# A Perceiver block on one core: the experts' first block prepared while self-attention drains

## What is computed

```python
x = x + cross_attention(layernorm(x), ctx, ctx, mask)      # 257 keys a batch, 16 heads
x = x + self_attention(layernorm(x))                       # 32 keys a batch, 16 heads
x = x + moe(layernorm(x))

def moe_layer(x, rw, rb, g, b, w1, b1, w2, b2):            # four of these in a row
    probs = softmax(x @ rw + rb)                           # 4 experts
    vals, idx = top_k(probs, 2); vals = vals / vals.sum()
    xhat = layernorm(x)
    xe = xhat * g[e] + b[e]                                # own gain and offset per expert
    h = gelu(xe @ w1[e] + b1[e])                           # 128 -> 512, exact gelu
    expert_out[e] = x + h @ w2[e] + b2[e]                  # 512 -> 128
    return sum over e of comb[e] * expert_out[e]           # all four are computed, two weigh
```

## Time and profile before

| | us |
|---|---|
| median of 3 executions | 1393.75 |
| lowest, highest | 1386.02, 1393.91 |
| the profiled execution | 1394.39 |
| its span, first to last instruction | 1391.7 |
| PE busy (share) | 1292.1 (93%) |
| DVE busy | 1167.6 (84%) |
| ACT busy | 1114.4 (80%) |
| POOL busy | 712.9 (51%) |

### The profile page before, as it was taken

How to read it: one execution, slowest core, us unless ns; L and a number is a source line. 1 busy time by engine, 2 the same in 40 slices (tenths; PEclk the granted TensorE clock), 3 DMA queues, 4 the chain that set the end, 5 groups by cost and what they waited for, 6 DMA issues and landing times.

```text
span 1391.7 us, 45724 instructions
## 1 busy us (share of the span) xinstructions
PE 1292.1 (93%) x15671; PEld 976.8 (70%) x15671; DVE 1167.6 (84%) x3416; ACT 1114.4 (80%) x1886; POOL 712.9 (51%) x557
## 2 busy tenths in 40 slices
PE   5898999999997699986999999999999999999998
PEld 3676778778776588843767667777777777777776
DVE  4799988999998689887999988788878887889885
ACT  3598999999996657655898978888888888888886
POOL 7276777777776865531444433333333333333333
PEclk9899999999998679997999999999999999999999
DMA  5875766766763288800000000000000000000000
GB/s 157 231 211 161 188 187 181 191 185 186 195 172 90 42 216 219 220 14 1 2 1 0 0 1 1 0 0 0 0 0 0 0 0 0 2 8 15 8 17 16
DMA packets 196207, 108.54 MB, mean 78 GB/s; under 512 B 89740, under 2 KB 194028, under 8 KB 196076
## 3 DMA queue, kind: packets, MB, share of 16 engines
q1 hardware_dynamic: 122032, 84.65, 21.9%
q10 hardware_dynamic: 74044, 22.17, 7.2%
HBM read 67.62 MB, written 39.03 MB: 77 GB/s over the span
## 4 chain that ended last, share of the span: by engine, by line
PE 46%; DVE 3%; issue 2%; ACT 1%; DVEq 0%; ACTq 0%
PE pair L1787 22%; PE pair L1769 20%; PE pair L1776 2%; PE pair L1808 1%; PE pair L1799 1%; DVE hs L1693 1%; ACT gf L1614 0%; DVE w1p L1046 0%; DVE gl L1679 0%; DVE w2p L1050 0%; DVE rw L38 0%; DVE st L1640 0%; DVE xl L1740 0%; ACT gh L1619 0%; DVE rs L53 0%
## 5 line engine op out<-in xcount | busy, mean ns | idle before, releaser
L1601 POOL TENSOR_TENSOR gl<-gf,gh 128x1024 f16<-128x1024 f32 x128 | 286.5, 2239 | 480.4 <-ACT gh L1619 480.4
L1614 ACT ACTIVATE gf<-pair,b1c 128x512 f32<-128x512 f32 x512 | 327.2, 680 | 98.3 <-PE pair L1769 97.0
L1787 PE MATMUL pair<-w2p,gh 128*128 (+1 forms) x4096 | 357.3, 219 | 0.0
L1787 PE MATMUL pair<-w2p,gl 128*128 (+1 forms) x2048 | 349.6, 219 | 0.0
L1769 PE MATMUL pair<-xh,w1p 128*128 128x512 f16 x1024 | 329.2, 383 | 9.8 <-ACT gf L1614 8.2
L1787 PEld LDWEIGHTS pair<-w2p,gh 128*128 128x128 f16 x4096 | 319.7, 98 | 23.0 <-issue 0.4
L405 POOL TENSOR_TENSOR pl<-p,ph 128x1024 f16<-128x1024 f32 x128 | 273.1, 2134 | 118.5 <-ACT ph L462 118.4
L1619 ACT ACTIVATE gh<-gf 128x1024 f16<-128x1024 f32 x256 | 270.6, 1057 | 24.0
L1679 DVE SCALAR_TENSOR_TENSOR gl<-gf,gh 128x1024 f16<-128x1024 f32 x128 | 160.8, 1256 | 83.5 <-ACT gh L1619 81.3
L1787 PEld LDWEIGHTS pair<-w2p,gl 128*128 128x128 f16 x2048 | 200.3, 98 | 0.0
L1769 PE MATMUL pair<-xl,w1p 128*128 128x512 f16 x512 | 196.1, 383 | 0.0
(11 more groups left out here) (240 smaller groups left out, 2448.8 us busy)
## 6 DMA issues: line engine op xcount, KB each, us to landing
KS<-k_parts_dram SPq DMA_DIRECT2D x64, 384.0 KB, 4.4
k_parts_dram<-kh SPq DMA_DIRECT2D x64, 256.0 KB, 3.4
cx<-in_ctx_dram ACTq DMA_DIRECT2D x30, 512.0 KB, 4.5
k_parts_dram<-kl SPq DMA_DIRECT2D x64, 128.0 KB, 3.6
w1p<-in_L_ffn_w_dram SPq DMA_DIRECT2D x8, 512.0 KB, 5.8
w2p<-in_L_ffn_w_dram SPq DMA_DIRECT2D x8, 512.0 KB, 7.6
QS<-q_parts_dram ACTq DMA_DIRECT2D x128, 24.0 KB
K<-k_parts_dram SPq DMA_DIRECT2D x8, 384.0 KB
```

The lines of the kernel that those rows point to most:

```text
L1601: pool.tensor_tensor(gl[u.m2][:, 0:h, :], gf[u.m2][:, 0:h, :], gh[u.m2][:, 0:h, :], ALU.subtract).then_inc(d_loP, 1)
L1614: act.activation(gf[u.m2][:, c, :], hb[c][:, :], ACT.Gelu, scale=1.0 / WS, bias=b1c[:, u.step.expert(u.e), c]).then_inc(d_g, 1)
L1787: last = pe.matmul(yb[v.m2][:, t * D:(t + 1) * D], g[:, c, t * P:(t + 1) * P], w2p[:, le, part, c, :].rearrange("p a h -> p (a h)"), start ...
```

## The change

It has four parts.

1. *The experts' first block in the drain.* DVE's aggregation and deviations of the first 24 tiles move two slots earlier, (7, 0) to (7, 2). ACT writes `hs` tiles 0 to 11 at the ends of slots (7, 3), (8, 0), (8, 1), tiles 12 to 15 in the prologue, and 16 to 31 in units (1, 1), (1, 3), (2, 1), (2, 3). DVE makes the moments of the first eight of these tiles in (8, 1) (`st8`, `mv8`), the deviations of steps 0 and 1 together and `xc` of step 0 in (8, 2), and PE transposes it at the end of the block. ACT issues one small GELU (`warm`) in (8, 0).
2. *The offsets' products with swapped operands.* For each expert four products with a 128x128 piece of fp32 weights as stationary and the one column of offsets as moving operand, written to where `b1c` reads them: `lnbd`, `b1r` and the transposes go. All sixteen experts are done in (6, 2) to (7, 3). The low weights of experts 0 and 1 are made by DVE in (7, 3) and (8, 0), and wait for all sixteen; those of 2 and 3 move to units (0, 0) and (0, 1).
3. *Routing behind the first unit.* In the prologue DVE only makes `xl` and `route` of step 0 and `xc` of step 1. The tanh moves behind the GELUs of unit (0, 0), `weigh` behind the low half there. `deviations(2)` is in (0, 2), behind `low_half(2)`; `attended_late` is at the end of (1, 2) and now makes only scales and biases.
4. *Steps 1 to 6 are written out* instead of looped.

```diff
-                            if at == (NBLK, 1):
-                                act.wait_ge(c_s, HEAD + 4)
-                                act.wait_ge(e_ln, HEAD + RSTD_STEPS + 1)
-                                for t in range(FIRST_HS):
-                                    attended(act, t)
-                            if at in ((NBLK, 1), (NBLK, 2)):
-                                high_weights(act, 1 + w)
...
+                            if at in ATTENDED:
+                                for t in range(*ATTENDED[at]):
+                                    attended(act, t)
+                            if at == (NBLK, 0):
+                                act.activation(warm[:, :], gain[:, 0:1], ACT.Gelu)
+                            if at in ((NBLK, 0), (NBLK, 1)):
+                                high_weights(act, 2 + w)
+                    ATTENDED = {(7, 3): (0, 4), (NBLK, 0): (4, 8), (NBLK, 1): (8, 12)}
...
-                            if at in ((7, 3), (NBLK, 1), (NBLK, 2), (NBLK, 3)):
-                                le = w % 4 if at[0] == NBLK else 0
-                                dve.wait_ge(e_b1, le + 1)
-                                low_weights(dve, le)
...
+                            if at in ((7, 3), (NBLK, 0)):
+                                le = (w + 1) % 4
+                                dve.wait_ge(e_b1, LE)
+                                low_weights(dve, le)
+                            if at == (NBLK, 1):
+
+                                dve.wait_ge(d_hs, 8)
+                                for k in range(8):
+                                    dve.bn_stats(st8[:, k, :], hs[:, k, :]).then_inc(d_ln, 1)
+                                dve.wait_ge(d_ln, 8)
+                                dve.tensor_tensor(b1c[:, :, :].rearrange("p x c -> p (x c)"), bank[1][:, 0:LE * FC],
+                                                  cols[:, 64:64 + LE * FC], ALU.add)
+                                for k in range(8):
+                                    dve.bn_aggr(mv8[:, k // 4, k % 4, :], st8[:, k, :]).then_inc(d_ln, 1)
+                            if at == (NBLK, 2):
+                                flat = lambda r: r[:, :, :].rearrange("p i k -> p (i k)")
+                                dve.wait_ge(d_ln, 16)
+                                inverse_deviation(dve, seed, flat(rs8), flat(rw8), flat(rt8),
+                                                  mv8[:, :, :, 1].rearrange("p i k -> p (i k)"), d_ln, 16)
+                                for k in range(4):
+                                    dve.tensor_scalar(xc[:, k, :], hs[:, k, :], mv8[:, 0, k, 0:1], rs8[:, 0, k:k + 1],
+                                                      ALU.subtract, ALU.mult).then_inc(d_x, 1)
...
-                                    pe.matmul(bank[1][0:LE, 0:F], lnbd[:, le, :], w1f[:, le + SHIFT, :], start=(le == 0),
-                                              stop=(le == LE - 1)).then_inc(e_b1, 1)
-                    BIAS1 = {(6, 2): (0, 1), (6, 3): (1, 2), (7, 0): (2, 3), (7, 1): (3, 4), (7, 2): (4, 6), (7, 3): (6, 8),
-                             (8, 0): (8, 10), (8, 1): (10, 12), (8, 2): (12, 14), (8, 3): (14, 16)}
+                                    for c in range(FC):
+                                        last = pe.matmul(bank[1][:, le * FC + c:le * FC + c + 1], w1f[:, le + SHIFT, c * P:(c + 1) * P],
+                                                         cols[:, 32 + le:33 + le], start=True, stop=True)
+                                    last.then_inc(e_b1, 1)
+                    BIAS1 = {(6, 2): (0, 2), (6, 3): (2, 4), (7, 0): (4, 7), (7, 1): (7, 10), (7, 2): (10, 13), (7, 3): (13, LE)}
...
-                with eng.Fori(0, SPLITS // 2) as it:
-                    for k in range(2):
-                        run(it, 1 + k, False, splits=True)
+                for s in range(1, 1 + SPLITS):
+                    run(0, s, False, splits=True)
...
-                        if f and e == 3:
-                            act.wait_ge(d_r, RSTEPS * (f.n + 1))
+                        weighed = u.step if at == (0, 0) else f if u and f and e == 3 else None
+                        if weighed:
+                            act.wait_ge(d_r, RSTEPS * (weighed.n + 1))
                             act.activation(th[:, :, :], z[:, :, :], ACT.Tanh).then_inc(d_th, 1)
...
+                    LATER = {(1, 1): (16, 20), (1, 3): (20, 24), (2, 1): (24, 28), (2, 3): (28, NT)}
...
                     def unit(u, v, f, third, e, final):
-                        if f and e == 0:
-                            if not u:
-                                deviations(f)
+                        at = (u.step.n, e) if u and isinstance(u.step.n, int) else None
+                        opening = at is not None and at[0] == 0
+                        if u and f and e == 0:
                             normalise(f, final)
-                        if third and e == 1 and u:
+                        if u and third and e == 1 and not opening:
                             deviations(third)
...
-                        if third and e == 1 and not u:
-                            deviations(third)
-                            attended_late()
                         if u:
                             low_half(u)
+                        if at == (0, 0):
+                            low_weights(dve, 2)
+                            weigh(u.step)
+                        if opening and e == 2:
+                            deviations(third)
                         if f and e == 2:
                             route(f)
                         if v:
                             combine(v, final)
...
+                        if at == (0, 1):
+                            low_weights(dve, 3)
+                        if at == (1, 2):
+                            attended_late()
```

More of the change, by code:

```diff
@@ L1060, in build @@
         e_rwh, e_b2, e_ln = sem("e_rwh"), sem("e_b2"), sem("e_ln")
-        d_acc = sem("d_acc")
+        st8 = sb(whole, "st8", [P, 8, 6], F32)
+        mv8 = sb(whole, "mv8", [P, 2, 4, 2], F32)
+        rs8, rw8, rt8 = (sb(whole, f"rs8_{i}", [P, 2, 4], F32) for i in range(3))
+        warm = sb(whole, "warm", [P, 1], F32)
+        xc = sb(whole, "xc", [P, 4, D], F32)
+        d_acc, d_hs = sem("d_acc"), sem("d_hs")
+        d_ln, d_x, d_xT = sem("d_ln"), sem("d_x"), sem("d_xT")
         def attended(act, t):
             act.activation(hs[:, t, :], xs[:, t, :], ACT.Identity, scale=rs3[:, t:t + 1],
-                           bias=nb3[:, t:t + 1]).then_inc(d_acc, E)
+                           bias=nb3[:, t:t + 1]).then_inc(d_hs, 1)
         with ExitStack() as S:
@@ L1089, in build @@
             cols = sb(S, "cols", [P, P], F32)
-            lnbd = sb(S, "lnbd", [P, LE, LE], F32)
-            b1r = sb(S, "b1r", [LE, F], F32)
             WLOAD = 16 * 2 * NBLK
@@ L1388, in step @@
                                              xs[:, bass.ds(y, 1), :].rearrange("p a c -> p (a c)")).then_inc(c_st, 1)
+                            if at in ((7, 0), (7, 1)):
+                                dve.wait_ge(c_st, NT + HEAD)
+                                for t in range(w * HEAD // 2, (w + 1) * HEAD // 2):
+                                    dve.bn_aggr(mv3[:, t, :], st2[:, t, :]).then_inc(e_ln, 1)
+                            if at == (7, 2):
+                                a = slice(0, HEAD)
+                                dve.wait_ge(e_ln, HEAD)
+                                inverse_deviation(dve, seed, rs3[:, a], rw3[:, a], rt3[:, a], mv3[:, a, 1], e_ln, HEAD)
+                                dve.scalar_tensor_tensor(nb3[:, a], mv3[:, a, 0], -1.0, rs3[:, a], ALU.mult, ALU.mult).then_inc(e_ln, 1)
@@ new lines, in step @@
+                                    last.then_inc(e_b1, 1)
+                    BIAS1 = {(6, 2): (0, 2), (6, 3): (2, 4), (7, 0): (4, 7), (7, 1): (7, 10), (7, 2): (10, 13), (7, 3): (13, LE)}
+                    blocks(step)(pe)
+                    pe.wait_ge(d_x, 4)
+                    pe.wait_ge(c_oc, NT)
+                    for k in range(4):
+                        last = pe.transpose(bank[6][:, k * P:(k + 1) * P], xc[:, k, :], ident[:, :])
+                    last.then_inc(d_xT, 1)
+        with ExitStack() as S:
+            st4 = st8[:, 0:4, :]
+            mv4, rs4, rw4 = ([t[:, i] for i in range(2)] for t in (mv8, rs8, rw8))
+            rt4 = rt8[:, 0]
+            sd4 = sb(S, "sd4", [P, 4], F32)
@@ L1547, in run @@
                     third = Step(eng, it, c + 2) if moments else None
-                    before = None if isinstance(it, int) and c == 0 or not attend else Step(eng, it, c - 1) if isinstance(it, int) else \
+                    before = None if isinstance(it, int) and c <= 0 or not attend else Step(eng, it, c - 1) if isinstance(it, int) else \
                         Before(it, c - 1)
@@ L1773, in outputs @@
                     def outputs(v):
-                        wait(pe, d_acc, 4 * v.n + (ACC0 - 4))
```

(5 more changed lines are left out.)

93 lines of the change are left out of this document (39 added, 54 removed).

## The result

| | before | after |
|---|---|---|
| median, us (4 executions each) | 1393.35 | 1410.59 |
| lowest, highest | 1386.02, 1393.91 | 1407.68, 1421.55 |
| ratio, 95% interval | | 1.0151, 1.0087 to 1.0214 |
| the profiled execution, its span | 1394.39, 1391.7 | 1410.22, 1408.4 |
| PE, DVE busy | 1292.1, 1167.6 | 1302.1, 1169.8 |

The changed kernel is 17 us slower. The prediction was 1393.0, with a range of 1385 to 1399, so it was wrong.

The account below looks back on a forecast made before the run. The prediction took DVE to bound layer 0 and PE the later layers. Its terms, 2.8 from the seam - 3.15 - 0.3 for attended_late + 1.4 for loops, gained 0.8 us: 1393.0 us, range 1385 to 1399.

Parts of the forecast that it names:

- What bounds the kernel: DVE sets the pace in layer 0, busy 22.80 of 23.70 us in a step; PE from layer 1 on.
- Drain: price of a swapped product: Offsets' products ahead of hidden 0: 0.90 us an expert after the swap, so the price does not change.
- Rival 4: Offsets' products in the drain cost twice, 1.7 us an expert, load and product in turn: 1406 us; chance 0.03.
- DVE's wait in (7, 3) and hidden 0: Drain's end: DVE waits for all sixteen experts' products, done at 620.4; hidden 0 starts at 635.4, 3.2 us later.
- First units: Behind hidden 0: ACT is no longer held, low_half(2) can start 7.5 us earlier, low_half(3) starts 2.8 earlier.
- The stand of PE: Before outputs(3): PE idles some 4 us, waiting for low_half(3).
- `attended_late`, 3.15 + 0.3: At (1, 2) in layer 0: 3.15 us of added DVE work and 0.3 for POOL, both lost.
- Loops, 1.4 gained: Steps 1 to 6: writing them out drops three idle pieces of DVE at loop ends, 1.4 us gained.
- Rival 1: Behind the seam DVE isn't the limit; ACT's 7.5 us stay, with 1.4 of the loops: 1385 us; chance 0.20.
- Rival 2: Clock falls to half after PE's stand before outputs(3), 4 to 4.5 us stay lost: 1397.5 us; chance 0.12.
- Rival 3: Swapped products in the drain are cheap, 0.3 us an expert: 1386 us; chance 0.08.
- The sum: Whole kernel: 2.8 - 3.15 - 0.3 + 1.4 = 0.8 us gained, a median of 1393.0 us.

Follow-up runs that it names:

- b_tiny: Kernel before with POOL's low half cut from 512 to 8 columns of each chunk, the rest left at zero: 1375.70 us, ratio 0.9875.
- wide: Changed kernel with each swapped offsets' product streaming 80 columns instead of one: 1401.88 us, ratio 1.0069.
- experiment 2: attended_late moved from (1, 2) to the end of the prologue, in the changed kernel (1408.04 us) and in wide (1398.91 us).
- wide_tiny: wide with POOL's low half cut from 512 to 8 columns of each chunk, the rest left at zero: 1370.88 us, ratio 0.9841.
- b_swap1: Kernel before with only the one-column swapped offsets' products, in their old slots: 1396.53 us, ratio 1.0029.
- b_swap80: Kernel before with only the swapped offsets' products, 80 columns wide, in their old slots: 1390.99 us, ratio 0.9981.
- b_routing80: Kernel before, loop kept, with 80-column swapped products in old slots, routing behind the first unit, attended_late and weigh behind low_half(0): 1388.41 us.
- b_unroll: Kernel before with the loop over split steps 1 to 6 written out, nothing else: 1398.14 us, ratio 1.0031.

## Why the prediction was wrong, step by step

**What bounds the kernel.** Right in the main: DVE in layer 0, and a microsecond lost there comes out at the end (+17.0 at `low_half(28)`, 16.7 of span). But the busy time that makes DVE the bound holds its blocks by POOL: without POOL's half it is busy 117.1 us from `low_half(3)` to `low_half(28)` in place of 139.1 (`b_tiny`). And it isn't the bound throughout once PE and ACT fall behind: in `wide` it waits 6.9 us for ACT there.

**Drain: price of a swapped product.** The step that failed. "At full clock 0.107 ... I take 0.90: the price does not change": at full clock it is right (24 pairs in 2.74 to 2.80 us, so 0.91 to 0.93 for eight), and reading full clock into a stretch whose PE work the change itself turns into one-column products was wrong: 0.213 a pair, 1.7 an expert. The row it came from the earlier trace rows had a clock of 0.50, and I scaled it away. Rival 4 had the size, 1.7 an expert, for another reason; its 13 us became 8 above the forecast, since only some batches ran at half clock.

**DVE's wait in (7, 3) and hidden 0.** Right, once the products' end is given. The prediction has 11.7 us from there to `xc`, short waits included, and 3.3 on to hidden 0. In `wide` the products end at 618.7 (620.4 forecast), `xc` is ready at 630.3 and hidden 0 starts at 633.49: 11.6 and 3.2. After the change it is 628.6, 640.3 and 643.45: 11.7 and 3.2.

**First units.** Right. ACT no longer waits for `z`, and the path from `xl(0)` to `low_half(2)` is 10.2 us shorter after and 10.1 in `wide`, against 3.2 + 7.5 = 10.7 forecast. From `low_half(2)` to `low_half(3)` the forecast had 11.5 with its meetings; 10.4 were measured in both. The stand of PE, forecast at some 4 us, was 2.8 in both (it ends at 671.48 after the change).

**`attended_late`, 3.15 + 0.3.** Right for DVE's busy time, 3.5 us in `wide`, and mis-sized as a whole: 6.1 us (experiment 2). What had no term is PE's stand of more than 4 us behind it with the lower clock that follows, after which DVE stands itself: 2.6 us. ACT's sixteen tiles, which I counted as nothing, can have a part in it; no run takes them away.

**Loops, 1.4 gained.** The wrong sign: the stall is gone (0.3 us before `xc` after the change) and the edit costs 5 us in the kernel before. With the loop DVE's half stays 0.01 to 0.03 us ahead of POOL's in every split step; without it DVE is 0.12 ahead in step 1 and 0.24 behind in step 2. By which path the loop held the two together isn't shown: the idle 0.6 us ahead of `xc` is the visible difference on DVE, but PE, ACT and POOL had their own copies of the loop too. The prediction asked who meets POOL in the moved work, but counted removed idle time as a gain without asking which of the existing contacts it turns round. The rule for it stood on the very page of the Trainium skill that I named ("SBUF — State Buffer", that the order of issue decides), and the row of 1.99 us was one such contact.

**The rivals.** Rival 1 (1385, ACT's chain kept) isn't met even without POOL's half: of 10.3 us `wide_tiny` keeps 4.5. DVE's own work takes a third of what is given back, and the meetings with POOL two thirds. Rival 2 (clock falls behind a stand of PE of about 4 us) came true in another place, 700 to 710 in step 1. Rival 3 is refuted, 0.9 an expert and no less. What no rival held was that two of them add, and that a step with a constant rhythm can change it.

**The sum.** Forecast -0.8 at `low_half(28)`, measured +17.0: 17.8 us, of which 8.5 came with the clock (as far as `low_half(2)`), -1.0 at `low_half(3)`, and 10.3 in the steps (12.3 against 2.05 forecast). For the latter there are two measured prices: the written-out steps, 6.3 to 7.6 off (4.9 to 6.2 in place of -1.4), and `attended_late`, 2.0 to 2.7 above its price. That they nearly fill the 10.3 proves nothing: the first price is from kernels whose loss is blocks alone, while the changed kernel has part of its loss in DVE's waits for ACT. No run has the changed kernel with its loop, or without ACT's tiles, so how the 10.3 divide stays open.

## What to carry to other kernels

Price a small product by the clock that it leaves behind: a stretch in which PE only loads weights and streams one column is "busy" and may still run at half clock, and streaming more columns there can be free. In a pipeline where DVE and POOL meet, write down for each contact who starts first and by how much; where that is a few hundredths of a microsecond, an edit of the loop that holds it, even one that only takes idle time away, can move a block of 2 us from an engine nobody waits for to the one that sets the pace. Edits ahead of the loop left the order alone in three kernels here. Compare traces from a point of their own, and not by the clock of the whole run. A wait that puts the order back has to be on the instruction that meets the other one, which may belong to another unit.

## What the hardware showed that I had not expected

- PE 34.00 of 34.00 us busy at a granted clock of 0.65 (0.50 from 618 to 626), with products of one column; 0.95 with 80 columns and the same number of products. The busy time that the profile lists doesn't tell the clock.
- In the batches of 24, an fp32 load of 128x128 with its product follows the one before at 0.114 us at full clock when 1 column streams, and at 0.117 when 80 do.
- A loop of split steps kept DVE 0.01 to 0.03 us ahead of POOL over six steps and in four kernels (before, `b_swap1`, `b_swap80`, `b_routing80`); written out, the same instructions drifted in and out of it (DVE's half in five steps of `b_unroll`: 2.97, 3.17, 1.22, 2.96, 3.15 us).
